# Four kinds of TensorE product get other distances between their operands in SBUF: six unused tensors are declared between the tensors of a three-stage transformer layer

## The reference, cut to what matters

```python
x = x + xattn(layernorm(x), ctx, mask, Wq, bq, Wk, bk, Wv, bv, Wo, bo)   # 16 heads of 32, 2 x 8192 context rows
    # k = ctx @ Wk.T + bk ; v = ctx @ Wv.T + bv ; softmax(q k^T / sqrt(32)) v ; @ Wo.T + bo
x = x + window_attn(layernorm(x), W_qkv, b_qkv, W_lat, b_lat, W_proj, b_proj)   # 7 keys a query
x = x + moe(layernorm(x), ...)
    # scores = sigmoid(h @ gate_w.T); each expert takes its best 128 tokens
    # eo = silu(xin @ gw.T + gb) * (xin @ up_w.T + up_b); eo = eo @ down_w.T + down_b    (512 -> 2048 -> 512)
    # plus a shared branch: silu(x @ sh_gate.T) * (x @ sh_up.T) @ sh_down.T              (512 -> 1024 -> 512)
```

## Time and profile before

| | |
|---|---|
| median of 3 runs | 2816.34 us (2814.86 to 2817.19) |
| profiled execution, its own time | 2814.52 us |
| its span, first to last instruction | 2812.7 us |
| TensorE busy (PE) | 2778.2 us, 99% |
| VectorE busy (DVE) | 2170.9 us, 77% |
| ScalarE busy (ACT) | 1722.5 us, 61% |
| keys and values | about 20 to 750 us |
| attention | about 750 to 1812 us |
| window attention, shared branch | about 1820 to 2208 us |
| experts | about 2208 to 2804 us |

### The profile page before, as it was taken

One profiled execution on the slowest core, in us unless ns is written; L12 is line 12 of the kernel. 1 busy time (PEld: TensorE's weight loads), 2 busy tenths in 40 slices (PEclk: granted clock), 3 DMA queues, 4 the chain that ended last, 5 costly groups with the idle time before them and its releaser, 6 DMA issues. The chain is left out here.

```text
span 2812.7 us, 37416 instructions
## 1 busy us (share of the span) xinstructions
PE 2778.2 (99%) x14157; PEld 1766.3 (63%) x14157; DVE 2170.9 (77%) x1600; ACT 1722.5 (61%) x2489; POOL 88.1 (3%) x43
## 2 busy tenths in 40 slices
PE   8999999999999999999999999999999999999998
PEld 5888888888644444444444444445544688888886
DVE  5544444444599999999999999856647898888986
ACT  4222122211499999999999999624621577677775
POOL 0000000000000000000000000000000400000000
PEclk9999999999999999999999999999999999999999
DMA  5555555555655555555555555321130699999995
GB/s 219 199 193 197 191 188 200 188 200 182 189 132 137 132 137 133 136 133 136 144 125 144 125 144 126 77 73 46 46 127 19 265 372 350 348 344 350 342 348 197
DMA packets 229104, 515.51 MB, mean 183 GB/s; under 512 B 18130, under 2 KB 84050, under 8 KB 199628
## 3 DMA queue, kind: packets, MB, share of 16 engines
q1 hardware_dynamic: 225372, 505.15, 56.8%
q0 software_dynamic: 3584, 8.39, 1.3%
HBM read 400.03 MB, written 113.44 MB: 183 GB/s over the span
## 5 line engine op out<-in xcount | busy, mean ns | idle before, releaser
L534 DVE TENSOR_TENSOR AC<-AC,PR 128x2048 f32<-128x2048 f32 x448 | 988.4, 2281 | 5.0 <-ACT PR L499 5.0
L499 ACT ACTIVATE PR<-PS 128x512 f32<-128x512 f32 x1024 | 567.6, 610 | 55.5 <-PE PS L421 43.2
L421 PEld LDWEIGHTS PS<-QS,KS 128*128 128x128 f32 x2048 | 364.9, 188 | 336.3 <-ACT PR L503 181.3
L421 PE MATMUL PS<-QS,KS 128*128 128x512 f32 x2048 | 563.7, 416 | 4.1 <-ACT PR L499 3.1
L503 ACT ACTIVATE PR<-PS 128x1024 f32<-128x1024 f32 x512 | 502.4, 1051 | 0.0
L432 PE MATMUL PS<-PR,VC 128*32 128x512 f32 x4096 | 493.3, 599 | 0.7 <-ACT PR L499 0.7
L929 DVE TENSOR_TENSOR WL<-RAW,WH 128x2048 fp32r<-128x2048 f32 x192 | 436.3, 2286 | 58.4 <-ACT WH L924 58.4
L736 ACT ACTIVATE KH<-PS,bk_s 128x512 fp32r<-128x512 f32 x128 | 88.3, 690 | 536.5 <-PE PS L792 536.2
L924 ACT ACTIVATE WH<-RAW 128x2048 fp32r<-128x2048 f32 x192 | 362.0, 1912 | 7.5 <-PE PS L1363 5.2
L631 DVE SCALAR_TENSOR_TENSOR KL<-PS,bk_s,KH 128x512 fp32r<-128x512 f32 x128 | 95.5, 749 | 258.5 <-ACT KH L736 258.5
L432 PEld LDWEIGHTS PS<-PR,VC 128*32 128x32 f32 x4096 | 106.9, 109 | 217.5 <-issue 172.3
(11 more groups left out here) (208 smaller groups left out, 3210.7 us busy)
## 6 DMA issues: line engine op xcount, KB each, us to landing
KS<-kh_d SPq DMA_DIRECT2D x256, 256.0 KB
RAW<-in_gw SPq DMA_DIRECT2D x64, 1024.0 KB, 5.4
RAW<-in_up_w SPq DMA_DIRECT2D x64, 1024.0 KB, 5.4
RAW<-in_down_w SPq DMA_DIRECT2D x64, 1024.0 KB, 5.4
kh_d<-KH SPq DMA_DIRECT2D x32, 1024.0 KB, 4.4
kl_d<-KL SPq DMA_DIRECT2D x32, 1024.0 KB, 6.5
v_d<-VS SPq DMA_DIRECT2D x128, 256.0 KB, 2.9
KS<-kl_d SPq DMA_DIRECT2D x128, 256.0 KB
```

The lines of the kernel that those rows point to most:

```text
L421: pe.matmul(PS[:, m % RING, :], KS[N % 2][:, j, t * P:(t + 1) * P], QS[bg % 2][:, j, :], start=True, stop=True).then_inc(s_s, 1)
L499: nc.scalar.activation(PR[tile % BUFS][:, 2 * hp + jj], PS[:, bank + jj, :], ACT.Exp, scale=SCALE).then_inc(s_exp, 1)
L534: v.tensor_tensor(a[i % 2][:], a[i % 2][:], p[:], ALU.add).then_inc(s_acc, 1)
```

## The change

Six tensors that nothing reads or writes are declared between others, of 32, 64 or 96 floats (128, 256 or 384 bytes of a partition). Everything declared behind one in the same stage moves up by that much. No instruction is added, removed or moved, on any engine, and no semaphore wait changes; only addresses do.

```diff
@@ -130,6 +130,7 @@
         KS = [attn.enter_context(nc.sbuf_tensor("KS0", [P, J, CK], F32R))]
+        PAD2 = attn.enter_context(nc.sbuf_tensor("PAD2", [P, 64], F32))
         QS = [attn.enter_context(nc.sbuf_tensor("QS0", [P, J, SQ], F32R))]
@@ -181,7 +182,10 @@
-            WKH, WKL, WVH, WVL = (sb(n, [P, DC, D], F32R) for n in ("WKH", "WKL", "WVH", "WVL"))
+            WKH, WKL = (sb(n, [P, DC, D], F32R) for n in ("WKH", "WKL"))
+            PAD0 = sb("PAD0", [P, 32])
+            WVH, WVL = (sb(n, [P, DC, D], F32R) for n in ("WVH", "WVL"))
+            PAD1 = sb("PAD1", [P, 32])
@@ -290,6 +294,7 @@
         KS.append(sb("KS1", [P, J, CK], F32R))
+        PAD3 = sb("PAD3", [P, 64])
         QS.append(sb("QS1", [P, J, SQ], F32R))
@@ -969,10 +974,12 @@
         SPARE = se("SPARE", [P, 512 - 4 * E])
+        PAD4 = se("PAD4", [P, 64])
         XEH, XEL = ([se(f"{n}{i}", [P, DC, CAP], F32R) for i in range(2)] for n in ("XEH", "XEL"))
         for i in range(4, PAIRS):
             weight_pair(i)
         GE, HE = ([se(f"{n}{i}", [CAP, 512]) for i in range(2)] for n in ("GE", "HE"))
+        PAD5 = se("PAD5", [P, 96])
         HTH, HTL = ([se(f"{n}{i}", [P, FT, CAP], F32R) for i in range(2)] for n in ("HTH", "HTL"))
```

## The result

The changed kernel takes 2832.37 us (median of 4 runs, 2830.31 to 2835.36), the kernel before 2816.55 us. The ratio is 1.0055, with a 95% interval of 1.004 to 1.007: 16 us slower, where no effect was forecast. The profiled execution has a span of 2830.5 us against 2812.7, so 17.8 us to find.

A forecast was written before the change was run, and what follows sets the result against it. TensorE's matmul pitch was taken as the bound, with VectorE equally full in attention and DMA following in the experts. All terms were 0: 2814.5 + 0 = 2814.5 us profiled, 2816 us as median, range 2780 to 2842.

The forecast's parts named there:

- no effect: Whole kernel: the new distances change nothing, 2811 to 2822 us, likeliest 2816 us; chance 0.60.
- slower rival: Fp32r streams settle only at distance 0: +3.5 ns x 5021 = 17.6 us, 2834 us, or up to 2856 us; chance 0.18.
- What bounds the kernel, and by how much it would be multiplied: TensorE's pitch bounds all stages, VectorE beside it in attention; 5021 moved matmuls outside the scores multiply any price.
- The value for the price, 0 ns: All moved fp32r products: another distance costs or gains 0 ns for each part, so the time stays 2816 us.
- a real weight load under an fp32r stream: Transposes' loads at distances 0, 96 and 416: next start 0.23 us later each time, taken as the nearest rows for 0 ns.
- the other two rows it used: Plain fp32 products at 96 and 0 both last 592 ns; one-column bias weights at odd address: bias follows in 0.22 us.
- The bias row: Bias weights, one column repeated, load under a stream at an odd address; bias follows in 0.22 us, like its neighbours.
- The stream settles at 226.7 ns whatever it starts from: Fp32r streams: after the bias, starts return from 0.24 us apart to 0.226, read as a cost independent of distance.
- The faster rival: Fp32r products: distance 0 is a bank clash losing 12.1 ns each; 2755 us in full, around 2785 in part; chance 0.22.

The follow-up runs named there:

- e8: Kernel before with distance 160 bytes modulo 256 in keys, values and, on WH0 to WH3, rows and hidden; scores and WH4 at 0: 2853.05 us, ratio 1.0135.
- e11: Separate trace-only kernel: one fp32r or transpose load at 0, 96, 128 or 160 under a settled distance-0 stream; fp32r at 96 gives 397 ns, at 0 389.
- e6: Separate trace-only kernel: streams at finer distances, with 64 weight columns, in plain fp32 and in alternating pairs; plain fp32 592 ns, pairs 390 to 392 ns.
- e10: Separate trace-only kernel: fp32r streams varying weight columns, one-word weights, one-word moving operand and alternating operands; the one-word moving stream lasts 381 ns.
- e1: Kernel before with 96 unused floats between WKL and WVH and 32 behind WVL, moving values alone to distance 384: 2826.59 us, ratio 1.0034.
- e2: Kernel before with 32 unused floats ahead of HTH0, moving the hidden products alone to distance 384: 2821.76 us, ratio 1.0017.
- e3: Kernel before with PAD0 and PAD2 to PAD5 of 64 floats, no PAD1: only distances 0 and 256 result; 2816.65 us, ratio 1.0.
- e5: Separate trace-only kernel: 48 fp32r matmuls at each of 32 distances, 0 to 496 bytes in steps of 16; 389 ns at 0, up to 397.

## Why the prediction was wrong

The measured 2832 us lies inside the stated 2780 to 2842, but the forecast was no effect, 2811 to 2822 us. What came is the slower rival, which had been given 0.14 in that range.

**What bounds the kernel, and by how much it would be multiplied: right.** TensorE's pitch is the price in keys, values and experts; e8 let 4867 slower matmuls through to the total without cover. Attention took 1062.0 us for 1061.6, as forecast, though no run made its matmuls slower.

**The value for the price, 0 ns: the step that failed.** It was taken from "a real weight load under an fp32r stream", that of the transposes, which did not differ at 0, 96 and 416. e11 repeats that comparison: the transposes' loads indeed do not tell distance, 392 to 394, but fp32r loads do, 389 at 0, 397 at 96, 396 at 128 and 391 at 160. The rows were read correctly and were the wrong kind: weights of plain fp32, loaded for a transpose, where the change moved fp32r weights of products (which of the two differences makes them blind, no run separates). Two things in the trace before could have warned. The timeline's starts are in steps of 10 ns, and the effect in question was at most 12; its unrounded starts do bear the reading out, 231.5, 231.8 and 230.8 ns in the mean at distance 0, 416 and 96. But that is 5 ns above the 226.7 of an fp32r load at the same distance 0, so a transpose's load was visibly another thing. The prediction named a difference between these two kinds of load as what would make it wrong, and still gave no effect 0.60. Beside it, the other two rows it used were of the same sort: plain fp32 products do not depend on distance (e6), and weights out of one word neither (e10, 394 at 0 and at 384). The bias row showed more than was read from it: the bias matmul behind that load, and the three after it, start 0.23 to 0.24 us apart. The prediction called this timing at one and the same distance; a disturbance from the load at the odd distance, carried on as in e11, would look the same, and no run tells them apart.

**"The stream settles at 226.7 ns whatever it starts from": true at distance 0 and 256, not at 384.** The slower rival doubted it, and that rival is what happened: at 384 the values' durations go on changing and average 395 ns (e1). Its price of +3.5 ns on 5021 matmuls, 17.6 us, met the 16 us, but by other terms: +6 ns on the values (1536 x about 6 = 10 us, e1) and on the hidden products (768 x about 6 = 4.6 us of the 5.2 that e2 measured, the rest on their neighbours), and 0 on keys and rows, for 256 is as good as 0 (e3). Too small a loss on too many matmuls: that the total fits is luck.

**The faster rival** started from a real loss, 12.1 ns in every fp32r matmul, and had the sign wrong: distance 0 is the good case, and of all distances tried with 128 weight columns none gave a mean under the 389 ns of the kernel before. The loss at the best distance is not one of distance; a stream over one word escapes 8 ns of it (218.7 ns), one over 512 words does not.

**The skill's rule.** The Trainium skill, "TensorE: Matmul & The Clock Gate" ("Step-by-step: what each phase is for"), has a weight load take nothing from the running matmul. e11 does not agree for fp32r: one load at 96 bytes costs the running matmul 8 ns.

What stays open is the mechanism inside: what in 256 bytes repeats, why 4 bytes off is harmless and 8 are not, why fewer weight columns lose more at distance 0 and less at 160, and whether a matmul's own weights and the step from one stream to the next count beside the load that runs meanwhile (e6, e10). No kernel here beats the one before; e5 found no distance that one could have been built on.

## What to carry to other kernels

Where a back-to-back stream of fp32r matmuls with 128 weight columns and 512 streamed columns bounds a kernel, keep the moving operand and the next weights at the same address modulo 256 bytes, which tensors of 512-byte multiples give for nothing; a small odd tensor declared between them cost up to 3.4% of that stage here (e8, 708.2 us for 685.2), and no busy share shows it, only the mean duration of the group or the count in a stretch. With 64 weight columns this rule fails (e6: 392 ns at 0, 389 at 160), so other shapes need a sweep of their own. When the trace has no row of the very thing that changes, a near row of another type bounds nothing: the case asks for a chance near even, not for 0.60.

## What was not expected of the hardware

- The duration of a matmul in an fp32r stream depends on distance with a period of 256 bytes, duration 389 ns at 0 and 4, 389 at 16 in one kernel and 390 in another, up to 397 at 160 (e5, e6). This is for 128 weight columns; with 64, 160 is the best of four distances at 389 ns and 0 the worst at 392 (e6).
- One fp32r load at 96 slows the matmul beside it and the two behind it, 397, 395 and 393 ns for 389 (e11).
- Plain fp32 matmuls show none of it, 592 ns at 0, 64, 128 and 160 (e6).
- 16 weight columns give a longer matmul than 128 at distance 0, 394 ns against 389 (e10).
- The distance slows matmuls with no other engine at work (e5) and within the layer, where DMA moves 341 GB/s in the experts of e8. So what clashes belongs to TensorE's own two operands; that it is their reads of SBUF is argued, not shown.
